# A mixture of experts' second layer as fp32r passes of high and low halves, feature-major, with the routing weights spread by transfers

## The reference

```python
normed = hidden_states * jax.lax.rsqrt(var + 1e-08) * norm_weight
shared = jnp.maximum(normed @ sw1 + sb1, 0.0) @ sw2 + sb2
probs = jax.nn.sigmoid(flat @ router_w.T)
scores, idx = jax.lax.top_k(probs, TOPK)
w = scores / (jnp.sum(scores, axis=-1, keepdims=True) + 1e-06)
comb = comb.at[jnp.arange(T)[:, None], idx].add(w)
h = jnp.maximum(jnp.einsum('td,edh->teh', flat, ew1) + eb1[None, :, :], 0.0)
eo = jnp.einsum('teh,eho->teo', h, ew2) + eb2[None, :, :]
routed = jnp.einsum('teo,te->to', eo, comb)
return shared + routed.reshape(b, s, -1)
x = x + _layernorm(_L0_ffn_ref(_layernorm(x, axis=-1), ...), axis=-1)
```

## Time and profile before

| | us |
|---|---|
| median of 3 runs | 2038.34 |
| lowest, highest | 2037.19, 2041.45 |
| the profiled execution | 2038.1 |
| its span | 2036.3 |
| mixture of experts, up(0) of chunk 0 to the last down | 852.5 to 1103.6 |

### The profile page before, as it was taken

The page is one execution under the profiler, slowest core; times in us unless marked ns, Lnnn a source line. Parts: engine busy times, 40 slices in busy tenths (PEclk is TensorE's granted clock), DMA queues, the critical chain, the costliest instruction groups (busy, mean ns, idle before and its releaser), DMA issues.

```text
span 2036.3 us, 37994 instructions
## 1 busy us (share of the span) xinstructions
PE 1941.5 (95%) x12066; PEld 1669.8 (82%) x12066; DVE 1518.0 (75%) x2604; ACT 1378.1 (68%) x2641; POOL 1122.8 (55%) x1361
## 2 busy tenths in 40 slices
PE   4999999999999999899998999999999999999688
PEld 3888888888888888689997788888888888888566
DVE  5988898889898989643223777777777777777575
ACT  3878787878787878544443677777777777776355
POOL 3655555555555555320001677777777777778521
PEclk9999999999999999999999999999999999999699
DMA  4212111111111111100000000000000000100000
GB/s 113 48 44 48 43 46 43 46 43 46 43 46 43 46 43 45 47 14 1 1 1 1 9 3 12 1 10 0 10 0 10 0 10 0 65 1 1 1 5 17
DMA packets 37766, 51.22 MB, mean 25 GB/s; under 512 B 8489, under 2 KB 17714, under 8 KB 37426
## 3 DMA queue, kind: packets, MB, share of 16 engines
q1 hardware_dynamic: 37682, 50.15, 9.7%
HBM read 15.52 MB, written 1.05 MB: 8 GB/s over the span
## 4 chain that ended last, share of the span: by engine, by line
PE 84%; DVE 6%; issue 4%; ACT 3%; POOL 2%; DMA 1%; SPq 0%; ACTq 0%; DVEq 0%; POOLq 0%
PE ps_t L546 7%; PE ps_o L556 7%; PE ps_t L1018 6%; PE ps_o L557 5%; PE ps_s L578 5%; PE ps_s L579 5%; PE ps_s L1354 5%; PE ps_s L1355 5%; PE ps_s L1356 5%; PE ps_t L1408 3%; PE ps_o L1422 3%; PE ps_o L1424 3%; PE ps_o L1423 3%; PE ps_s L999 2%; PE ps_s L1000 1%
## 5 line engine op out<-in xcount | busy, mean ns | idle before, releaser
L1558 DVE TENSOR_REDUCE a_negmax<-ps_s 128x1 f32<-128x1024 f32 x256 | 312.4, 1220 | 67.3 <-PE ps_s L1356 64.7
L720 DVE TENSOR_REDUCE a_negmax<-ps_s 128x1 f32<-128x1024 f32 x256 | 313.5, 1224 | 52.5 <-PE ps_s L579 37.7
L1486 ACT ACTIVATE a_p<-ps_s,a_negmax 128x1024 f32<-128x1024 f32 x256 | 286.5, 1119 | 95.2 <-DVE a_negmax L1558 94.1
L655 ACT ACTIVATE a_pth<-ps_t 128x512 fp32r<-128x512 f32 x512 | 278.7, 600 | 91.4 <-PE ps_t L546 91.2
L706 DVE TENSOR_TENSOR a_ptl<-ps_t,a_pth 128x512 fp32r<-128x512 f32 x512 | 327.6, 681 | 6.5 <-ACT a_pth L655 5.5
L783 POOL TENSOR_SCALAR a_p<-a_p,a_rsum 128x1024 f32<-128x1024 f32 x256 | 289.4, 1130 | 52.8 <-POOL a_rsum L779 52.8
L1659 POOL TENSOR_TENSOR a_p<-a_p 128x1024 f32<-128x1024 f32 x128 | 307.7, 2404 | 10.7
L779 POOL TENSOR_TENSOR a_rsum<-a_sum,minus_one 128x1 f32<-128x1 f32 x256 | 141.4, 552 | 306.7 <-ACT a_p L685 305.5
L685 ACT ACTIVATE a_p<-ps_s,a_negmax 128x1024 f32<-128x1024 f32 x256 | 288.6, 1127 | 15.2 <-DVE a_negmax L720 15.2
L546 PEld LDWEIGHTS ps_t<-ident_r,a_pr 128*128 128x128 f32 x2048 | 200.4, 140 | 32.0 <-POOL a_p L783 4.0
L556 PE MATMUL ps_o<-a_pth,a_v 128*128 128x512 f32 x512 | 220.4, 431 | 3.6 <-ACT a_o L664 2.2
(11 more groups left out here) (228 smaller groups left out, 4537.7 us busy)
## 6 DMA issues: line engine op xcount, KB each, us to landing
a_q<-a_kh SPq DMA_DIRECT2D x64, 128.0 KB, 2.2
a_q<-a_kl SPq DMA_DIRECT2D x64, 128.0 KB, 2.3
a_kh<-a_kh SPq DMA_DIRECT2D x64, 128.0 KB, 2.2
a_kl<-a_kl SPq DMA_DIRECT2D x64, 128.0 KB, 2.3
a_w_raw<-in_l_w SPq DMA_DIRECT2D x8, 384.0 KB, 3.0
f_raw<-in_ffn_w SPq DMA_DIRECT2D x2, 1408.0 KB, 7.8
f_w_raw<-in_ffn_w SPq DMA_DIRECT2D x9, 256.0 KB, 5.7
f_w<-in_ffn_w SPq DMA_DIRECT2D x9, 256.0 KB, 4.3
```

Of the source, the lines that this page charges most:

```text
L720: dve.tensor_reduce(a0_negmax[:, s % 4:s % 4 + 1], ps_s[:, s % 2, :, :], AX.XY, ALU.max, negate=True)\
L1558: dve.tensor_reduce(a1_negmax[:, s % 2, m:m + 1], ps_s[:, m, :, :], AX.XY, ALU.max, negate=True)\
```

## The change

- **Second layer.** w2 and h are split in halves: `f0_w2_hi` (ACT) and `f0_w2_lo` (POOL), made in chunk 0 for all nine experts; for h ACT reads each bank and writes h (`f0_h`, fp32), and for the first two tiles of features also the high half `f0_hh`; for the last two POOL rounds h (`high`). DVE subtracts, `f0_hl` = h - hh, in the place of h (`low`). down(pos) is 4 x 3 fp32r passes with w2 stationary and 512 tokens moving: feature-major output.
- **Sums.** The weights are per token, now along the free axis: combT goes to DRAM and comes back as rows spread over 128 partitions (`f0_combB`, three slots). DVE multiplies (`f0_yw`) and adds (`f0_yT`), 128x512 each. Bias: one fp32 matmul of 512 columns. At the end of a chunk PE turns `f0_yT` back with four transposes (`f0_pe_y`) and ACT copies it to Y (`f0_act_y`), at position 1 of the next chunk, for chunk 3 at the start of the second attention.
- **DVE's order.** At each position DVE makes the four subtractions and then the sum of the position two before. The norm's stages 1 to 3 of chunk 1 come before low(0, 0), stage 4 after it; the routing's half 0 after low(0, 1); half 1 in chunk 1, in two parts after low(1, 0) and low(1, 1).
- **Norms.** After chunks 0 to 2 the scalings and the sum with x go to POOL (`x1_apply`), the statistics stay on DVE at positions 2 and 4 of the next chunk. After chunk 3 all stays as it was.
- **POOL in chunk 0**, per position: high, w2_lo, w1_lo of two positions later; in chunks 1 to 3: high.
- The transposes and router products of chunks 2 and 3 come one position later (7 and 8). The loops over chunks on ACT, DVE and POOL are written out. The load of b1 comes after the first attention's last product, before w2. Buffers lie elsewhere, the first attention's too.

```diff
+        f0_w2_hi = sb("f0_w2_hi", [P, NE, HT, D], F32R)
+        f0_w2_lo = sb("f0_w2_lo", [P, NE, HT, D], F32R)
+        f0_hh = [[sb(f"f0_hh{i}{j}", [P, BANK], F32R) for j in range(HT)] for i in range(2)]
...
+        f0_hl = [[sb(f"f0_hl{i}{j}", [P, BANK], F32R) for j in range(HT)] for i in range(2)]
...
         def f0_sp(sp):
             sp.wait_ge(S["a0_pv"], 4 * H0)
+            sp.dma_start(f0_b1[:, :, :], t["ffn0_b1"]).then_inc(S["f0_b1_loaded"], 16)
             for pos in range(NE):
...
+            for c in range(NC):
+                sp.wait_ge(S["f0_combT_ready"], c + 1)
+                sp.dma_start(comb_dram[c], f0_combT[:, :]).then_inc(S["f0_combT_stored"], 16)
+                sp.wait_ge(S["f0_combT_stored"], 16 * c + 16)
+                sp.sem_inc(S["waited"], 1)
+                for pos in range(1, NE):
+                    if c * NE + pos > 3:
+                        sp.wait_ge(S["f0_weighted"], c * NR + max(pos - 3, 0))
+                    e = f0_expert(pos)
+                    sp.dma_start(f0_combB[pos % 3][:, :], comb_dram[c, e:e + 1, :].broadcast_to([P, BANK]))\
+                        .then_inc(S["f0_combB_in"][pos % 3], 16)
+                if c == 0:
+                    a1_load_first(sp)
...
                 def down(pos):
-                    pe.wait_ge(S["f0_relued"], c * (NE * HT) + HT * (pos + 1))
                     if pos < 2:
-                        pe.wait_ge(S["f0_added"], c * NE)
+                        pe.wait_ge(S["f0_weighted"], c * NR)
                     elif pos == 2:
                         pe.wait_ge(S["f0_shared"], c + 1)
                     else:
-                        pe.wait_ge(S["f0_added"], c * NE + (pos - 1))
...
-                    for i in range(TPC):
-                        for ht in range(HT):
-                            ins = pe.matmul(ps_t[:, pos % 2, i * P:(i + 1) * P], f0_h[pos % 2][ht][:, i * P:(i + 1) * P],
-                                            f0_w2[:, pos, ht, :], start=ht == 0, stop=ht == HT - 1)
+                        pe.wait_ge(S["f0_weighted"], c * NR + (pos - 2))
+                    if start:
+                        pe.wait_ge(S["f0_w2_lo_ready"], pos + 1)
+                    bank = ps_t[:, pos % 2, :]
+                    for ht in range(HT):
+                        pe.wait_ge(S["f0_hl_ready"], c * (NE * HT) + (HT * pos + ht + 1))
+                        w_hi, w_lo = f0_w2_hi[:, pos, ht, :], f0_w2_lo[:, pos, ht, :]
+                        pe.matmul(bank, w_hi, f0_hh[pos % 2][ht][:, :], start=ht == 0, stop=False)
+                        pe.matmul(bank, w_hi, f0_hl[pos % 2][ht][:, :], start=False, stop=False)
+                        ins = pe.matmul(bank, w_lo, f0_hh[pos % 2][ht][:, :], start=False, stop=ht == HT - 1)
                     ins.then_inc(S["f0_down"], 1)
...
+                        src, bias = ps_s[:, ht // 2, ht % 2, :], f0_b1[:, f0_expert(pos), ht:ht + 1]
+                        ins = act.activation(f0_h[pos % 2][ht][:, :], src, ACT.Relu, bias=bias)
+                        if ht < 2:
+                            ins = act.activation(f0_hh[pos % 2][ht][:, :], src, ACT.Relu, bias=bias)
+                        ins.then_inc(S["f0_relued"], 1)
+                    if start:
+                        f0_act_w2_hi(act, pos)
...
+            def low(c, pos):
+                for ht in range(HT):
+                    if ht < 2:
+                        dve.wait_ge(S["f0_relued"], c * (NE * HT) + (HT * pos + ht + 1))
+                    else:
+                        dve.wait_ge(S["f0_hh_ready"], (c * NE + pos) * 2 + (ht - 1))
+                    dve.tensor_tensor(f0_hl[pos % 2][ht][:, :], f0_h[pos % 2][ht][:, :], f0_hh[pos % 2][ht][:, :], ALU.subtract)\
+                        .then_inc(S["f0_hl_ready"], 1)
...
             def add_expert(c, pos):
                 dve.wait_ge(S["f0_down"], c * NE + (pos + 1))
+                dve.wait_ge(S["f0_combB_in"][pos % 3], 16 * f0_slot_uses(c, pos))
                 dve.wait_ge(S["f0_added"], c * NE + pos)
...
+                dve.tensor_tensor(f0_yw[:, :], ps_t[:, pos % 2, :], f0_combB[pos % 3][:, :], ALU.mult)\
+                    .then_inc(S["f0_weighted"], 1)
+                dve.wait_ge(S["f0_weighted"], c * NR + pos)
+                dve.tensor_tensor(f0_yT[:, :], f0_yw[:, :], f0_yT[:, :], ALU.add).then_inc(S["f0_added"], 1)
...
+            for c in range(1, NC):
+                n = NORM_F0 + 2 * (c - 1)
+                for pos in range(NE + 2):
+                    if pos < NE:
+                        low(c, pos)
+                    if pos >= 2:
+                        if pos == 2:
+                            add_bias(c)
+                        else:
+                            add_expert(c, pos - 2)
+                    if c == 1 and pos < 2:
+                        f0_dve_route(dve, 1, pos)
+                    if pos == 2:
+                        dve.wait_ge(S["f0_y_out"], c)
+                        norm_stats(dve, n, 0, lambda k: y_tile((c - 1) * TPC + k))
+                    if pos == 4:
+                        dve.wait_ge(S["x1_summed"], c)
+                        norm_stats(dve, n + 1, 1, lambda k: x_tile((c - 1) * TPC + k))
...
+            for pos in range(NE):
+                high(0, pos)
+                f0_pool_w2_lo(pool, pos)
+                if pos < NE - 2:
+                    f0_pool_w1_lo(pool, pos + 2)
...
+            for c in range(1, NC):
+                for pos in range(NE):
+                    high(c, pos)
+                    if pos in (2, 4):
+                        x1_apply(pool, c - 1, pos // 2 - 1)
...
+        def x1_apply(pool, c, i):
+
+            norm_rstd(pool, NORM_F0 + 2 * c + i, i)
...
+            for k in range(TPC):
+                x, y = tile(X, c * TPC + k), tile(Y, c * TPC + k)
+                dst, src = (tile(xhat, k), y) if i == 0 else (y, x)
+                ins = pool.tensor_scalar(dst, src, mv[:, i, k, 0:1], rstd[:, i, k:k + 1], ALU.subtract, ALU.mult)
...
         def a1_pe(pe):
             spare = ps_t[:, 1, :]
 
+            f0_pe_y(pe, NC - 1)
+            pe.wait_ge(S["f0_y_out"], NC)
```

More of the change, by code:

```diff
@@ L165, in sandwich_kernel @@
         a1_sq = sb("a1_sq", [P, DV1])
+        f1_raw = sb("f1_raw", [P, 2 * HID + 2 * HT * HID + HT * D])
+        f1_s = sb("f1_s", [P, 4 * HT + 1])
         sb(None, LOW)
@@ L937, in f0_act_probs, with f0_dve_route @@
                            scale=-1.0).then_inc(S["f0_exped"], 1)
-        def f0_dve_route(dve, half):
+        def f0_dve_route(dve, half, part):
             def step(ins):
@@ L948, in f0_dve_route @@
             rank = f0_rank[:, :].rearrange("p (a e) -> p a e", a=1).broadcast_to([P, n, NR])
-            dve.wait_ge(S["f0_exped"], half + 1)
-            step(dve.tensor_scalar(f0_tmp[:, t, :], f0_prob[:, t, :], 1.0, None, ALU.add))
-            step(dve.reciprocal(f0_prob[:, t, :], f0_tmp[:, t, :]))
-            for k, p in ((0, f0_prob), (1, f0_left)):
+            if part == 0:
+                dve.wait_ge(S["f0_exped"], half + 1)
+                step(dve.tensor_scalar(f0_tmp[:, t, :], f0_prob[:, t, :], 1.0, None, ALU.add))
+                step(dve.reciprocal(f0_prob[:, t, :], f0_tmp[:, t, :]))
+            for k, p in (((0, f0_prob),), ((1, f0_left),))[part]:
                 step(dve.tensor_reduce(f0_top[k][:, t], p[:, t, :], AX.X, ALU.max))
@@ new lines, in f0_pe_y, with f0_act_y @@
+        def f0_pe_y(pe, c):
+            pe.wait_ge(S["f0_added"], c * NE + NE)
+            for i in range(TPC):
+                ins = pe.transpose(ps_m[:, i * P:(i + 1) * P], f0_yT[:, i * P:(i + 1) * P], ident[:, :])
+            ins.then_inc(S["f0_y_turned"], 1)
+        def f0_act_y(act, c):
+            act.wait_ge(S["f0_y_turned"], c + 1)
+            y = Y[:, c * TPC:(c + 1) * TPC, :].rearrange("p t d -> p (t d)")
+            act.activation(y, ps_m[:, :], ACT.Copy).then_inc(S["f0_y_out"], 1)
@@ L1050, in chunk @@
                         f0_pe_logits(pe, 1)
-                    if start and pos == 7:
+                    if start and pos == 8:
                         f0_pe_logits(pe, 2)
@@ L1059, in chunk @@
                         bias()
-                    if start and pos == 6:
+                    if pos == 1 and not start:
+                        f0_pe_y(pe, c - 1)
+                    if start and pos == 7:
                         pe.wait_ge(S["f0_added"], 1)
@@ L1100, in f0_act @@
             f0_act_w1_hi(act, 1)
-            chunk(0, True)
-            with act.Fori(1, NC) as c:
-                chunk(c, False)
+            act.wait_ge(S["f0_b1_loaded"], 16)
+            for c in range(NC):
+                chunk(c, c == 0)
         def f0_dve(dve):
@@ new lines, in add_expert @@
+                dve.wait_ge(S["f0_weighted"], c * NR + pos)
+                dve.tensor_tensor(f0_yT[:, :], f0_yw[:, :], f0_yT[:, :], ALU.add).then_inc(S["f0_added"], 1)
+            y_tile = lambda k: tile(Y, k)
+            x_tile = lambda k: tile(X, k)
```

(19 more changed lines are left out.)

173 lines of the change are left out of this document (85 added, 88 removed).

## The result

The changed kernel takes 2072.74 us (median of 4 runs, 2070.68 to 2074.91), the kernel before 2039.89 on the same chip: ratio 1.0162, 95% interval 1.0146 to 1.0178, slower by 33 us. The forecast was 2045.0, slower, in a range that ended at 2057. The profiled execution is the longest of the four, 2074.91 us with a span of 2073.0.

What follows compares the result with a forecast made beforehand. The prediction took PE to bound the kernel (84% of the span). Chunk 0 +13.3, chunk 1 -1.2, chunks 2 and 3 -3.95 each, hand-over +2.75 sum to +6.95 us on 2038.1: 2045.0 us, range 2028 to 2057.

Steps and rivals of the forecast that it cites:

- PE work, -6.8 us a chunk: All chunks: shorter down passes, less the turn of the summed output, save PE 6.8 us a chunk, 27 us in all.
- the fourth rival: Second layer not shorter: down passes at 0.29 us, PE gain gone, waits stay, 2072 us; chance 0.02.
- the third: Rival: broadcast loads come late, each chunk pays some 5 us at 15 us a load, 2065 us; chance 0.07.
- Four tiles at 0.375: POOL's four norm scalings at 0.375 us each; the norm on POOL then costs 1.35 us a later chunk, 1.05 before down(3).
- The 1.5 before down(8): End of chunks 1 to 3: down(8) could start at T+5.6 but waits for DVE's product until T+7.1, 1.5 us.
- -3.95: Chunks 2 and 3, each: PE saving of 6.8 us less waits of 1.5 and 1.35 us.
- Chunk 1, -1.2 forecast: Chunk 1: PE saving of 6.8 us less waits of 1.5, 1.35 and, for the moved routing, 2.75 us.
- Chunk 0, +13.3 forecast: Chunk 0: DVE and POOL wait each other out; +8.8 us to the end of its bias, +4.5 us for the rest.
- DVE first and POOL first: Chunk 0 behind its bias: 50 us if DVE goes first at each tie, 55.4 if POOL does; 52.7 taken.
- The first rival: DVE and POOL do not block each other where it matters; chunk 0 ends 3.5 us earlier, 2028 us; chance 0.22.
- Hand-over, +2.75 forecast: Hand-over to the second attention: turn and copy of Y and later weight transposes delay the scores by 2.75 us.
- PE idle over 4 us in each later chunk: Sign named beforehand, chunks 1 to 3: PE idle over 4 us would mean the position schedule is mis-worked.

Runs made afterwards that it cites:

- e9: Changed kernel with the norm's scalings and sum back on DVE, and in chunks 1 to 3 the weighted sum ahead of the subtractions: 2044.6 us, ratio 1.0032.
- e15: Changed kernel with POOL's norm scaling as add and mult, both with a scalar per partition (computes other values): 2063.9 us, ratio 1.0121.
- e16: Changed kernel with POOL's norm scaling as mult and mult, both with a scalar per partition (computes other values): 2061.6 us, ratio 1.0118.
- e6: Changed kernel with POOL's subtractions for the weights' low halves replaced by a single short memset each, low halves left out: 2057.9 us, ratio 1.0109.
- e7: Changed kernel with DVE's norm stage 4 of chunk 1 placed between the first and last two subtractions of position 0: 2070.1 us, ratio 1.0159.
- e8: Changed kernel with PE's transposes of the second attention's weights ahead of the turn of Y, in free banks: 2068.2 us, ratio 1.0152.
- e5: Changed kernel with POOL's subtractions for the weights' low halves replaced by two memsets each, similar in time, reading no SBUF: 2059.0 us, ratio 1.0102.
- e10: e9 with norms, turns and router products of chunks 2 and 3 moved to chunk 1, their routing to chunk 2: 2040.6 us, ratio 1.0015.
- e14: e10 plus the edits of e7 and e8, with ACT writing all rounded halves of h and POOL none, in all chunks: 2025.3 us, ratio 0.9939.
- e1: Kernel before the change with only the change's buffer places: 2039.6 us, ratio 1.0007.

## Why the forecast missed

The sign held, for the reason given in chunk 0 and the hand-over; the gain expected in chunks 1 to 3 did not come, and the cost was 33 us instead of 7. In the profiled execution the excess over the forecast, 2074.9 less 2045.0 = 29.9 us, lies as follows.

- **PE work, -6.8 us a chunk: right.** e9's chunk 2, all PE at the upper clock, is 7.1 us shorter than before. Passes are 0.23 us apart, so the fourth rival is out, and so is the third: the broadcasts land in 3.2 us.
- **"Four tiles at 0.375": the step that failed first.** They took 0.79 us each. I took a row with mult and mult for one with subtract and mult, and nothing in the trace of before showed the difference. 1.35 us a chunk became waits of 3.60 and 0.96 in chunk 2. With 0.447 a tile (e15, e16) the wait before down(3) was still 1.77, not 1.05, so the price of the subtraction is 1.8 of these us, and the clock behind the wait comes on top. The 1.5 before down(8) was 1.29, closer than the forecast's rows allow: roundings out at T+4.65 and 5.2 and subtractions 0.61 apart end at T+5.9, not 6.5, which makes that wait 0.9. Waits together: 3.0 us more than forecast in chunks 2 and 3 each.
- **The clock behind a wait was left out of chunks 1 to 3**, though the forecast had it, once, in chunk 0. After 3.60 us without a pass the granted clock was at its lower level. PE's busy time is 2.4 and 2.6 us above e9's 51.9 in chunks 2 and 3 and 6.3 us in chunk 1. With the waits this gives the +1.2 and +1.4 measured where -3.95 was forecast.
- **Chunk 1, -1.2 forecast, +8.7 measured.** Its waits were 3.40 (routing, 2.75 forecast), 4.67 before down(3) and 1.29, 9.4 in all against 5.6; the clock's 6.3 us come on top. Adding the routing's delay to the norm's was right: the waits without the routing's are 6.0 us, against 5.85 in chunk 2. The single 4.67 us belongs to this execution: in e6, e7 and e8, whose code is the same here, the waits are 3.7 before down(3) and 0.9 before down(5). Chunk 1 takes 65.4 to 66.3 us in those, so a part of the clock's 6.3 belongs to this execution too.
- **Chunk 0, +13.3 forecast, +18.1 measured.** The mechanism was right and e5 shows it: POOL's reads beside DVE make up to 12.4 us, the lower clock behind the waits included. The size was off in both parts: 36.3 against 34.7 us to the end of the bias, and 56.0 against 52.7 behind it, where I took the middle between DVE first and POOL first and the chip gave POOL first (55.4) and a little more. In the rows above POOL begins its subtraction 0.5 us after DVE's pair, and both take longer.
- **The first rival had the wrong zero.** It held that without exclusion chunk 0 would be 3.5 us shorter than before; e5 and e6 measured 5.8 and 4.5 longer. Its zero left nothing for DVE's own order of norms, routing and halves, nor for POOL's roundings in front of them. e10 (11.6 us by moving norms away) and e14 point there, but both still had the exclusion, so how the 5.8 us divide is open.
- **Hand-over, +2.75 forecast, +3.7 measured**; e8 confirms the mechanism, transposes behind the copy, for about 2 us of it.
- **The start, costed at nothing**: +4.0 in this execution, by e1 scatter for a good part, with some 2 us for the new places not excluded.

Sum, for chunks 0 to 3, hand-over and start: 4.8 + 9.9 + 5.2 + 5.4 + 0.9 + 4.0 = 30.2; the stages behind took 0.4 us less than before. "PE idle over 4 us in each later chunk would mean that the position schedule is mis-worked" was the line that came true.

## What to carry to other kernels

Work that is moved to another engine has to be costed by a row with the same operation, not the same shape; where no such row is there, the bound must be a multiple, not the nearest one. When PE depends on a second engine in every position, look at what stands in front of the late instruction in that engine's own order: putting the consumer's sum ahead of the next position's subtractions was worth 13 us and cost nothing. And a wait on PE can be priced twice, once as a wait and once as the passes at the lower clock behind it: here that was so behind nearly every wait over 2.5 us and behind about half of those of 1.5 to 2.3.
